# Three edge walks of a graph network with their hardware loops written out, and tile loads without bounds checks

## The chip, the cores and the metric

One core of one Trainium2 chip runs the whole program in a single launch. The metric is device time in microseconds (us) of that core. The kernel before took 7643.01 us in the median of 3 runs (7601.51 to 7684.22).

## What is computed

A graph of N = 3125 nodes (256 features each) and E = 53125 directed edges, self loops among them, goes through eight residual blocks, `x = x + block(layernorm(x))`: two graph convolutions, slice attention, graph attention (GAT), a mixture of experts, an edge update with a GRU, a second mixture, a relational convolution and a third mixture. The change touches two of them, graph attention and the edge update:

```
# graph attention, H = 4 heads of C = 64
h = (x @ W).reshape(N, H, C)
a_s = einsum('nhc,hc->nh', h, att_src);  a_d = einsum('nhc,hc->nh', h, att_dst)
e = leaky_relu(a_s[src] + a_d[dst], 0.2)
p = exp(e - segment_max(e, dst)[dst])
alpha = p / segment_sum(p, dst)[dst]
agg = segment_sum(h[src] * alpha[:, :, None], dst)

# edge update (row = src, col = dst)
msg = relu(concat(h[row], h[col], edge_attr) @ W1.T + b1) @ W2.T + b2
agg = segment_sum(msg, row)          # then a GRU over the nodes
```

## The kernel before

Nodes lie in 25 tiles of 128 (`NT`), a node per partition. The edges are sorted once by target node (and once by source, for the edge update) into WT = 440 columns of 128 slots; every column belongs to one node tile, whose number is read at run time from the rows `m.tn1` and `m.tn2`. The index of each slot's far node is in `m.src1`, its place within the tile in `m.lo1`.

An **edge walk** goes over the 440 columns in order, four (Q) at a time; such a four is a quad, and there are 110 (`QUADS`). Per column POOL gathers 128 rows of a table in DRAM by an indirect DMA, DVE builds a one-hot matrix from `lo1`, PE multiplies the one-hot matrix with the rows, so that the rows of each node are added up (or spread), and DVE adds or compares the result into the tile's place in SBUF. The engines run their own instruction streams, tied by semaphores; each has an order of steps written out by hand. The three walks that are changed:

- the **max walk** (lines 1408 to 1518) finds the greatest source score per node and head: POOL `gather` of `table_max` (L1453), ACT `masks` (L1436, L1439), PE `spread` (L1470, L1472), DVE `greatest` (L1501), `first_heads` (L1490), `hots` (L125), `keep` (L1512);
- the **sum walk** (1521 to 1677) weights and adds up the rows: POOL `gather` of `table_gat` (L1569), PE `turn_hots` (L1583), `scores` (L1592), `sums` (L1600), ACT `turned_hots` (L1550) and `numerators` (L1555), DVE `exponents` (L1641 to L1653), `weigh` (L1660, L1661), `add` (L1671);
- the **edge walk** (2116 to 2263) of the edge update: SP loads the slots' records, ACT copies their indices out (L2152), POOL gathers (L2183), PE `turn_in` (L2198, L2200), `inner` (L2211, L2212), `sums` (L2220), DVE `hots`, `mix` (L2249), `add` (L2258).

`pipeline(eng, ring, *steps)` (L143) orders one engine's steps. A step `(ahead, f)` is issued for quad q + ahead in the turn of quad q. The turns before quad 0 are written out; then a hardware loop (`Fori`) runs 110 // 8 - 1 = 12 rounds of 8 turns, in which quad numbers are register values, so that waits compare with a register and addresses are computed; the remaining 14 turns (quads 96 to 109) are written out with constants. In the attention walks ACT's step `indices`, six quads ahead, copies a quad's four index columns from `m.src1` at a register offset to a small ring `idx`, after PE is done with the quad eight before; POOL's `gather` waits for that copy, raises a semaphore `issue` that nobody waits for, and issues four gathers.

The node tile numbers come into registers through `node_tiles` (L163): one load of 8 numbers in every second quad for `NodeTiles` (DVE in all three walks, PE in the sum walk), one of 4 per quad for PE's `inner` in the edge walk. With each number goes a register instruction and an assert that check 0 to 24. `aggregate` (L612), which the graph convolutions (twice) and the relations use, is another edge walk, fully written out, with constant waits, indices read in place and tile numbers loaded through `tile_registers` (L605), without the checks.

Of the kernel before, what the change touches and what calls it, by code (L numbers as in the profile page):

```python
# [21 lines left out]
I32 = mybir.dt.int32  # L22
# [117 lines left out]
        return self.tiles[u % 2 * Q:(u % 2 + 1) * Q]  # L140


def pipeline(eng, ring, *steps, total=QUADS):  # L143

    rounds = total // ring - 1

    def turn_of(q):
        for ahead, step in steps:
            if 0 <= q + ahead < total:
                step(q + ahead, (q + ahead) % ring, (q + ahead) // ring)  # L150

    assert all(0 <= ahead <= ring for ahead, _ in steps)
    for q in range(-max(ahead for ahead, _ in steps), 0):
        turn_of(q)
    with eng.Fori(0, rounds) as i:
        for u in range(ring):
            for ahead, step in steps:
                step(i * ring + (u + ahead), (u + ahead) % ring, i + (u + ahead) // ring)
    for q in range(rounds * ring, total):
        turn_of(q)  # L160


def node_tiles(nc, eng, tn):  # L163

    return nc.values_load_multi_w_load_instructions(tn, engines=[eng.engine], min_val=0, max_val=NT - 1)[1]


def setup_memory(nc, ctx):
# [1151 lines left out]
def graph_attention(nc, m, a):  # L1320
# [85 lines left out]


    with Stage(nc) as st:
        names = ("indexed", "hot", "masked", "made", "topped", "bested", "issue", "initial")
        indexed, hot, masked, made, topped, bested, issue, initial = (st.sem(s) for s in names)  # L1410
        R, RS = 8, 4
        gathered = st.sems("gathered", R * Q)
        S = view(m.WS, 0, RS * Q, P)
        off = view(m.WS, RS * Q * P, RS * Q * P // 2).bitcast(BF16).rearrange("p (u e) -> p u e", e=P)
        o = RS * Q * P * 3 // 2
        rows = view(m.WS, o, R * Q, H)
        idx = view(m.WS, o + R * Q * H, R * Q).bitcast(I32)
        top = view(m.WS, o + R * Q * (H + 1), 2 * Q, H)
        minus = m.WS[:, o + R * Q * (2 * H + 1):o + R * Q * (2 * H + 1) + 1]
        diag = high[:, 0:RS * Q * H * P].rearrange("p (u h e) -> p u h e", u=RS * Q, h=H)  # L1420
# [2 lines left out]

        @block.scalar
        def _(act):
            def indices(j, u, r):
                act.wait_ge(made, j + 1)
                nc.scalar.copy(idx[:, u * Q:(u + 1) * Q], m.src1[:, bass.ds(j * Q, Q)]).then_inc(indexed, 1)

            def masks(j, u, r):  # L1430
                k = u % RS
                act.wait_ge(made, j + 1 + R - RS)
                for s in range(Q):
                    act.wait_ge(gathered[u * Q + s], r * 16 + 16)
                    for h in range(1, H):
                        nc.scalar.mul(diag[:, k * Q + s, h, :], m.ident[:], rows[:, u * Q + s, h:h + 1])  # L1436
                act.wait_ge(hot, j + 1)

                nc.scalar.activation(off[:, k * Q:(k + 1) * Q, :], S[:, k * Q:(k + 1) * Q, :], ACT.Identity,  # L1439
                                     bias=minus, scale=MASK).then_inc(masked, 1)  # L1440

            act.wait_ge(initial, 2)
            pipeline(act, R, (6, indices), (2, masks))

        @block.gpsimd
        def _(pool):
            nc.gpsimd.memset(minus, -MASK).then_inc(initial, 1)
            nc.gpsimd.tensor_copy(best, src_score).then_inc(initial, 1)
            def gather(j, u, r):
                pool.wait_ge(indexed, j + 1)  # L1450
                pool.sem_inc(issue, 1)
                for q in range(u * Q, (u + 1) * Q):
                    nc.gpsimd.indirect_dma_start(rows[:, q, :], None, m.table_max,  # L1453
                                                 bass.IndirectOffsetOnAxis(ap=idx[:, q:q + 1], axis=0)
                                                 ).then_inc(gathered[q], 16)

            pipeline(pool, R, (0, gather))

        @block.tensor
        def _(pe):  # L1460
            pe.sem_inc(made, R)

            def spread(j, u, r):
                k = u % RS
                pe.wait_ge(masked, j + 1)
                pe.wait_ge(topped, j + 1)
                for s in range(Q):

                    at = m.PS[:, u % 2 * Q + s, :]
                    nc.tensor.matmul(at, off[:, k * Q + s, :], m.identb[:].unsqueeze(1).to_broadcast([P, H, P]),  # L1470
                                     start=True, stop=False)
                    mm = nc.tensor.matmul(at, S[:, k * Q + s, :], diag[:, k * Q + s].rearrange("p h e -> p (h e)"),  # L1472
                                          start=False, stop=True)
                mm.then_inc(made, 1)

            pipeline(pe, R, (0, spread))

        @block.vector
        def _(dve):
# [25 lines left out]
            def keep(s):  # L1505

                def step(j, u, r):
                    if s == 0:
# [5 lines left out]


            node_tile, tiles = NodeTiles(nc, dve, m.tn1), [None] * Q
            pipeline(dve, R, (0, greatest), (2, first_heads), (0, keep(0)), (2, hots), (0, keep(1)), (0, keep(2)),
                     (0, keep(3)))


    with Stage(nc) as st:
        names = ("dstep", "ready", "own_diffed", "own_expd", "selfed", "indexed", "hot", "turned", "tcopied",
                 "scored", "taken", "estep", "diffed", "expd", "weighted", "summed", "added", "issue")
        (dstep, ready, own_diffed, own_expd, selfed, indexed, hot, turned, tcopied, scored, taken, estep, diffed,
         expd, weighted, summed, added, issue) = (st.sem(s) for s in names)
        R, RT = 8, 4
        gathered = st.sems("gathered", R * Q)
        S = view(m.WS, 0, R * Q, P)
        ST = view(m.WS, R * Q * P, RT * Q, P)
        o = (R + RT) * Q * P  # L1530
        idx = view(m.WS, o, R * Q).bitcast(I32)
        e, lk, p = (view(m.WS, o + (1 + k * H) * R * Q, R * Q, H) for k in range(3))
        own = view(m.WS, o + (1 + 3 * H) * R * Q, NT, H)
        rows = view(high, 0, R * Q, RW)
# [5 lines left out]

        @block.scalar
        def _(act):
            def indices(j, u, r):
                act.wait_ge(summed, (j + 1) * Q)
                nc.scalar.copy(idx[:, u * Q:(u + 1) * Q], m.src1[:, bass.ds(j * Q, Q)]).then_inc(indexed, 1)  # L1545
# [15 lines left out]
            pipeline(act, R, (6, indices), (4, turned_hots), (2, numerators))  # L1561

        @block.gpsimd
        def _(pool):
            def gather(j, u, r):
                pool.wait_ge(indexed, j + 1)
                pool.sem_inc(issue, 1)
                for q in range(u * Q, (u + 1) * Q):
                    nc.gpsimd.indirect_dma_start(rows[:, q, :], None, m.table_gat,  # L1569
                                                 bass.IndirectOffsetOnAxis(ap=idx[:, q:q + 1], axis=0)  # L1570
                                                 ).then_inc(gathered[q], 16)

            pipeline(pool, R, (0, gather))

        @block.tensor
        def _(pe):
# [29 lines left out]
            pipeline(pe, R, (2, scores), (0, sums), (4, turn_hots))  # L1606

        @block.vector
        def _(dve):
# [67 lines left out]
            pipeline(dve, R, (4, hots), (1, weigh), *mixed)  # L1677


    with Stage(nc) as st:  # L1680
# [417 lines left out]
def edge_update(nc, m, a):  # L2098
# [10 lines left out]
    def keep(dst):  # L2109
        return lambda t, ps: nc.vector.tensor_copy(tile_at(dst, t), ps)  # L2110
# [5 lines left out]
    CW = D + 1  # L2116
    with Stage(nc) as st:
        names = ("loaded", "oned", "indexed", "hot", "turned", "tcopied", "made", "mixed", "active", "summed",
                 "added", "issue")
        loaded, oned, indexed, hot, turned, tcopied, made, mixed, active, summed, added, issue = (  # L2120
            st.sem(s) for s in names)
        R, RS = 8, 4
        gathered, came = st.sems("gathered", RS * Q), st.sems("came", R)
# [14 lines left out]
        def _(sp):  # L2138
# [4 lines left out]
                sp.wait_ge(summed, (j + 1) * Q)  # L2143
                sp.dma_start(rec[:, u * Q:(u + 1) * Q, :], r[:, bass.ds(j * Q, Q), :]).then_inc(came[u], 16)

            pipeline(sp, R, (0, records))

        @block.scalar
        def _(act):
# [14 lines left out]
                nc.scalar.activation(rows[:, k, 0:D], rows[:, k, 0:D], ACT.Relu).then_inc(active, 1)  # L2164

            act.sem_inc(tcopied, 1)
            pipeline(act, R, (6, indices), (2, turned_in), (1, relu))

        @block.gpsimd
        def _(pool):  # L2170
# [6 lines left out]
            def gather(j, u, r):  # L2177
                pool.wait_ge(indexed, j + 1)
                pool.wait_ge(summed, (j + 1 + R - RS) * Q)
                pool.sem_inc(issue, 1)  # L2180
# [7 lines left out]
            pipeline(pool, R, (0, gather))  # L2188

        @block.tensor  # L2190
        def _(pe):
# [33 lines left out]
            pe.wait_ge(loaded, 16)  # L2225
            pe.wait_ge(oned, 1)
            pe.wait_ge(blanked, 2)
            pipeline(pe, R, (2, turn_in), (1, inner), (0, sums))

        @block.vector  # L2230
        def _(dve):
# [28 lines left out]
            dve.sem_inc(added, Q)  # L2260
            dve.sem_inc(mixed, 1)
            node_tile = NodeTiles(nc, dve, m.tn2)
            pipeline(dve, R, (3, hots), (1, mix), (0, add))


    sumsT = view(m.BB, 0, KD, NP)
# [745 lines left out]
```

## Time and profile before

| | |
|---|---|
| median of 3 runs | 7643.01 us (7601.51 to 7684.22) |
| the profiled execution | 7593.7 us, span 7591.9 us |
| PE busy | 5303.6 us (70%), mean granted clock 0.83 |
| DVE busy | 3536.6 us (47%) |
| POOL busy | 3390.8 us (45%) |
| ACT busy | 1465.3 us (19%) |
| max walk, sum walk, edge walk | 735, 775 and 770 us long |

The profile is of one execution. Times are us from the start of its span. A group's row gives busy time and mean ns of one instruction, then the idle time of the engine just ahead of it and what ended it; "issue" is idle time for which the profile shows no releaser. PEld is the weight load of a matmul. PEclk is the granted TensorE clock as a share of full speed (2.4 GHz). Register, branch and semaphore instructions have no rows of their own. The names of DMA releasers are those of an earlier stage that used the same semaphore, where stages share its number.

### The profile page before, as it was taken

What the parts mean: (1) busy time and instruction counts of PE and PEld (TensorE: products, weight loads), DVE (VectorE), ACT (ScalarE), POOL (GpSimd) and SP (SyncE); (2) the same over time, 40 slices, a digit from 0 to 9 for tenths busy, and PEclk for the clock granted to TensorE, in tenths of its full rate; (3) what the DMA queues carried; (4) which work ended last, traced back from release to release, by engine and by line L of the source; (5) the groups of instructions that cost most, each with busy time, mean ns of one, the idle gap of its engine ahead of it and who ended that gap; (6) DMA issues with size and microseconds to landing.
All of it is one profiled execution on the core that took longest, in us unless ns stands there. A gap on an engine that the chain in (4) does not pass through costs nothing. (4 is left out here: it accounts for less than half of the span.)

```text
span 7591.9 us, 94398 instructions
## 1 busy us (share of the span) xinstructions
PE 5303.6 (70%) x22797; PEld 3525.6 (46%) x22798; DVE 3536.6 (47%) x8494; ACT 1465.3 (19%) x3866; POOL 3390.8 (45%) x3530
## 2 busy tenths in 40 slices
PE   2665877677768477767776299479998549677645
PEld 0113555355535233335565188467776334355434
DVE  7874334333445466655556211355565632233412
ACT  0001000100032366631111122123333211000011
POOL 1714665466500266656662355335561030566322
PEclk9886888788889599977767599799999879788777
DMA  3102333233200000022321267323331043333245
GB/s 150 49 9 73 90 90 73 74 90 90 73 13 0 21 1 1 1 52 78 82 79 40 85 206 219 100 87 96 99 98 40 1 133 122 96 91 90 54 125 173
DMA packets 402907, 597.08 MB, mean 79 GB/s; under 512 B 131055, under 2 KB 305711, under 8 KB 401647
## 3 DMA queue, kind: packets, MB, share of 16 engines
q0 software_dynamic: 147584, 361.63, 17.2%
q1 hardware_dynamic: 255088, 232.69, 10.2%
q8 instruction: 103, 1.69, 0.1%
q14 instruction: 132, 1.08, 0.0%
HBM read 472.89 MB, written 121.17 MB: 78 GB/s over the span
## 5 line engine op out<-in xcount | busy, mean ns | idle before, releaser
L641 PE MATMUL ps<-zerow,zerob 128*128 128x256 bf16 x5280 | 966.1, 299 | 353.1 <-issue 301.4
L629 POOL DMA_INDIRECT wide<-table,src x880 | 884.1, 1005 | 733.5 <-ACTq L94 331.9
L671 DVE TENSOR_TENSOR sums<-sums,ps 128x256 f32 x1320 | 555.6, 421 | 1261.9 <-PE ps L644 775.2
L644 PE MATMUL ps<-wide 128*128 128x256 f32 x2640 | 947.2, 434 | 167.2 <-issue 152.1
L641 PEld LDWEIGHTS ps<-zerow,zerob 128*128 128x128 bf16 x5280 | 552.6, 107 | 749.4 <-issue 503.8
L629 POOL DMA_INDIRECT wide<-table_rel,rel x440 | 444.1, 1009 | 417.5 <-ACTq L94 217.6
L1569 POOL DMA_INDIRECT wide<-table_gat,work x440 | 469.6, 1067 | 309.9 <-ACT work L1545 174.2
L644 PEld LDWEIGHTS ps<-wide 128*128 128x128 f32 x2640 | 472.9, 217 | 277.8 <-issue 238.6
L2183 POOL DMA_INDIRECT work<-table,work x440 | 439.8, 999 | 306.0 <-PE ps L2220 158.2
L1453 POOL DMA_INDIRECT work<-table_max,work x440 | 432.9, 984 | 267.2 <-issue 138.7
L1472 PE MATMUL ps<-wide,work 128*128 128x512 f32 x880 | 499.5, 652 | 0.0
L1600 PE MATMUL ps<-wide,work 128*128 128x260 f32 x880 | 356.2, 562 | 91.5 <-DVE sums L1671 74.9
L1436 ACT ACTIVATE wide<-ident,work 128x128 f32<-128x128 f32 x1320 | 397.6, 387 | 4.3 <-DMA work<-table_max,work 4.0
L590 PE MATMUL ps<-ident,work 128*128 128x128 f32 x650 | 114.5, 341 | 368.2 <-ACT work L579 366.2
L1501 DVE TENSOR_REDUCE work<-ps 128x16 f32<-128x2048 f32 x110 | 252.0, 2291 | 194.6 <-issue 131.8
L486 POOL DMA_INDIRECT rec<-sums,record x256 | 248.5, 971 | 201.6 <-DMA sums<-in_edge_attr 128.6
L455 PE MATMUL ps<-wide 128*128 128x440 f16 x832 | 248.2, 392 | 113.7 <-DVE wide L431 55.3
L2211 PE MATMUL ps<-wide 128*128 x880 | 279.8, 401 | 60.2 <-DVE work L2249 36.6
L1671 DVE TENSOR_TENSOR sums<-sums,ps 128x260 f32 x440 | 186.7, 424 | 283.4 <-issue 100.8
L1470 PE MATMUL ps<-identb,work 128*128 128x512 bf16 x440 | 183.9, 418 | 191.8 <-ACT work L1439 170.0
L1600 PEld LDWEIGHTS ps<-wide,work 128*128 128x128 f32 x880 | 226.2, 277 | 164.7 <-DVE sums L1671 88.9
L579 ACT COPY work<-sums 128x256 f32 x100 | 33.6, 402 | 1378.9 <-PEq L583 1378.1
(431 smaller groups left out, 9347.1 us busy)
## 6 DMA issues: line engine op xcount, KB each, us to landing
wide<-in_L_ffn_W SPq DMA_DIRECT2D x64, 1024.0 KB
wide<-in_L_ffn_expert_w SPq DMA_DIRECT2D x90, 256.0 KB
table_rel<-wide SPq DMA_DIRECT2D x20, 1024.0 KB
work<-rows_in SPq DMA_DIRECT2D x62, 256.0 KB
rows_out<-work SPq DMA_DIRECT2D x62, 256.0 KB
work<-rec SPq DMA_DIRECT2D x110, 136.0 KB
wide<-table,src POOLq DMA_INDIRECT x880
rec<-work POOLq DMA_DIRECT2D x6, 2176.0 KB
```

Of the source, the lines that this page charges most:

```text
L629: nc.gpsimd.indirect_dma_start(rows[:, w % RT, :], None, table, bass.IndirectOffsetOnAxis(ap=index[:, w:w + 1], axis=0)).then_inc(gathered ...
L641: nc.tensor.matmul(m.PS[:, w % (2 * Q), 0:D], m.zerob[:, 0:P], m.zerow[:, 0:D], start=True, stop=True)
L644: nc.tensor.matmul(m.PS[:, w % (2 * Q), 0:D], S[:, w % RT, :], rows[:, w % RT, :], start=True, stop=True).then_inc(summed, 1)
L671: v.tensor_tensor(at, at, m.PS[:, s, 0:D], ALU.add).then_inc(added, 1)
L1436: nc.scalar.mul(diag[:, k * Q + s, h, :], m.ident[:], rows[:, u * Q + s, h:h + 1])
L1453: nc.gpsimd.indirect_dma_start(rows[:, q, :], None, m.table_max, bass.IndirectOffsetOnAxis(ap=idx[:, q:q + 1], axis=0)).then_inc(gathered[ ...
L1472: mm = nc.tensor.matmul(at, S[:, k * Q + s, :], diag[:, k * Q + s].rearrange("p h e -> p (h e)"), start=False, stop=True)
L1501: v.reduce_max(top[:, half * Q:(half + 1) * Q, :], m.PS[:, half * Q:(half + 1) * Q, :].rearrange("p s (h e) -> p s h e", h=H), AX).then_in ...
L1569: nc.gpsimd.indirect_dma_start(rows[:, q, :], None, m.table_gat, bass.IndirectOffsetOnAxis(ap=idx[:, q:q + 1], axis=0)).then_inc(gathered[ ...
L1600: te.matmul(m.PS[:, 4 + s, 0:RW], S[:, u * Q + s, :], rows[:, u * Q + s, :], start=True, stop=True).then_inc(summed, 1)
L2183: nc.gpsimd.indirect_dma_start(rows[:, k, 0:D], None, m.table, bass.IndirectOffsetOnAxis(ap=idx[:, u * Q + s:u * Q + s + 1], axis=0)).then ...
L2211: te.matmul(at, ST[:, k, :], tile_at(by_src, tiles[s]), start=True, stop=False)
```

## The change

`written_out` takes the place of `pipeline` in the three walks: the same turns in the same order, all 110 written out, so every quad number is a constant. `node_tiles` loads without the checks. In the attention walks ACT's step `indices`, the ring `idx` and the semaphores `indexed` and `issue` are gone, and POOL's gathers read their index column in `m.src1` itself. For the first eight quads a gather waits for nothing; later ones wait for the count that ACT's copy waited for. In the edge walk the index copy stays.

```diff
+def written_out(ring, *steps, total=QUADS):
+    for q in range(-max(ahead for ahead, _ in steps), total):
+        for ahead, step in steps:
+            if 0 <= q + ahead < total:
+                step(q + ahead, (q + ahead) % ring, (q + ahead) // ring)
...
 def node_tiles(nc, eng, tn):
-    return nc.values_load_multi_w_load_instructions(tn, engines=[eng.engine], min_val=0, max_val=NT - 1)[1]
+    return nc.values_load_multi_w_load_instructions(
+        tn, engines=[eng.engine], min_val=0, max_val=NT - 1,
+        skip_runtime_bounds_check_because="a count of node tiles started, ...")[1]
... (max walk)
-            def indices(j, u, r):
-                act.wait_ge(made, j + 1)
-                nc.scalar.copy(idx[:, u * Q:(u + 1) * Q], m.src1[:, bass.ds(j * Q, Q)]).then_inc(indexed, 1)
-
-            pipeline(act, R, (6, indices), (2, masks))
+            written_out(R, (2, masks))
             def gather(j, u, r):
-                pool.wait_ge(indexed, j + 1)
-                pool.sem_inc(issue, 1)
-                for q in range(u * Q, (u + 1) * Q):
+                if j >= R:
+                    pool.wait_ge(made, j + 1)
+                for s in range(Q):
+                    q, w = u * Q + s, j * Q + s
                     nc.gpsimd.indirect_dma_start(rows[:, q, :], None, m.table_max,
-                                                 bass.IndirectOffsetOnAxis(ap=idx[:, q:q + 1], axis=0)
+                                                 bass.IndirectOffsetOnAxis(ap=m.src1[:, w:w + 1], axis=0)
                                                  ).then_inc(gathered[q], 16)
-            pipeline(pool, R, (0, gather))
+            written_out(R, (0, gather))
-            pipeline(pe, R, (0, spread))
+            written_out(R, (0, spread))
... (DVE alike; the sum walk alike, with pool.wait_ge(summed, (j + 1) * Q); the edge walk:)
-            pipeline(sp, R, (0, records))
+            written_out(R, (0, records))
-            pipeline(act, R, (6, indices), (2, turned_in), (1, relu))
+            written_out(R, (6, indices), (2, turned_in), (1, relu))
             def gather(j, u, r):
                 pool.wait_ge(indexed, j + 1)
                 pool.wait_ge(summed, (j + 1 + R - RS) * Q)
-                pool.sem_inc(issue, 1)
-            pipeline(pool, R, (0, gather))
+            written_out(R, (0, gather))
-            pipeline(pe, R, (2, turn_in), (1, inner), (0, sums))
+            written_out(R, (2, turn_in), (1, inner), (0, sums))
-            pipeline(dve, R, (3, hots), (1, mix), (0, add))
+            written_out(R, (3, hots), (1, mix), (0, add))
```

## Rows read from the trace of the kernel before

**Rows 1.** Stretches of the max, sum and edge walks, and of a written-out walk.
```profile
core 0: us, PE busy (x) PEld busy (x) DVE busy (x) ACT busy (x) POOL busy (x), PEclk, DMA share, GB/s
2585.00:3320.00 735.00, 546.97 (x1320) 225.52 (x1320) 438.30 (x769) 474.65 (x1540) 433.19 (x442) 0.89 0.05 1
3330.00:4105.00 775.00, 549.20 (x2200) 433.30 (x2200) 440.58 (x1219) 100.13 (x331) 469.60 (x440) 0.71 0.30 77
4995.00:5765.00 770.00, 685.31 (x3521) 578.03 (x3522) 448.21 (x772) 236.33 (x443) 442.00 (x443) 0.96 0.34 95
6488.00:7135.00 647.00, 484.36 (x2513) 322.79 (x2514) 233.78 (x471) 0.00 (x0) 444.08 (x440) 0.82 0.33 90
```

**Rows 2.** Stretches, columns as before: looped, then written-out quads, of each walk.
```profile
2680.40:3191.70 511.30, 395.77 (x963) 163.41 (x962) 318.78 (x560) 345.04 (x1121) 315.06 (x321) 0.90 0.05 1
3241.50:3290.90 49.40, 38.88 (x97) 16.18 (x96) 31.43 (x56) 34.00 (x112) 30.65 (x31) 0.90 0.07 2
3421.00:3957.00 536.00, 398.60 (x1602) 315.46 (x1601) 312.39 (x881) 73.21 (x240) 337.40 (x321) 0.72 0.30 79
4014.40:4063.80 49.40, 38.74 (x156) 30.91 (x154) 30.88 (x89) 6.61 (x24) 33.15 (x33) 0.68 0.36 82
5070.10:5618.70 548.60, 498.32 (x2573) 420.98 (x2571) 325.90 (x561) 170.98 (x320) 320.56 (x321) 0.97 0.34 97
5672.90:5724.30 51.40, 46.81 (x246) 40.15 (x247) 32.13 (x56) 16.93 (x32) 31.68 (x32) 1.00 0.34 99
```

**Rows 3.** Timeline (start us, us, ...) of DVE's L1501: looped, then written-out quads.
```profile
3177.48 2.29 DVE L1501 TENSOR_REDUCE work<-ps 128x16 f32<-128x2048 f32 x1 [2.86 <-issue]
...
3191.76 2.29 DVE L1501 TENSOR_REDUCE work<-ps 128x16 f32<-128x2048 f32 x1 [3.81 <-issue]
...
3195.97 2.29 DVE L1501 TENSOR_REDUCE work<-ps 128x16 f32<-128x2048 f32 x1
...
3263.91 2.29 DVE L1501 TENSOR_REDUCE work<-ps 128x16 f32<-128x2048 f32 x1 [2.72 <-issue]
...
3272.84 2.29 DVE L1501 TENSOR_REDUCE work<-ps 128x16 f32<-128x2048 f32 x1 [4.67 <-PE ps L1472]
```

**Rows 4.** Groups of instructions of the max walk: POOL's gathers, ACT's index copies.
```profile
L1453 POOL DMA_INDIRECT work<-table_max,work x440 | 432.9, 984 | 267.2 <-issue 138.7 <-ACT work L1428 128.6
...
L1428 ACT COPY work<-src 128x4 int32 x96 | 17.0, 177 | 0.0
```

**Rows 5.** Waits in the sum walk: us in total, times, longest us.
```profile
POOL wide L1569 <- ACT work L1545: 174.2, 36, 45.5
```

**Rows 6.** Timeline of DVE: unchecked load in `aggregate`, checked load in the edge walk.
```profile
6809.14 1.22 DVE L125 TENSOR_TENSOR wide<-iota,lo 128x1024 f32<-128x1024 f32 x1
6811.77 0.42 DVE L671 TENSOR_TENSOR sums<-sums,ps 128x256 f32 x1 [1.42 <-issue]
...
5731.76 1.22 DVE L2249 TENSOR_TENSOR work<-work,ps 128x1024 f32<-128x1024 f32 x1 [2.71 <-DMA normed_T<-rows_out,back]
5734.83 0.42 DVE L2258 TENSOR_TENSOR sums<-sums,ps 128x257 f32 x1 [1.84 <-issue]
```

**Rows 7.** DMA queues: looped max walk; `aggregate`; last 91 us of the max walk.
```profile
q0 software_dynamic: 10829, 0.71, 4.8%
...
q8 instruction: 20, 0.33, 0.2%
q14 instruction: 14, 0.11, 0.1%
...
q14 instruction: 5, 0.04, 0.1%
```

**Rows 8.** Waits in `aggregate` (relations).
```profile
PE ps L641 <- issue: 101.3, 126, 3.1
...
POOL wide L629 <- PE ps L644: 56.1, 70, 2.8
...
POOL wide L629 <- DMA normed<-rows_out,back: 40.9, 31, 5.4
```

More of the change, by code:

```diff
@@ L163, in node_tiles @@
 def node_tiles(nc, eng, tn):
-    return nc.values_load_multi_w_load_instructions(tn, engines=[eng.engine], min_val=0, max_val=NT - 1)[1]
+    return nc.values_load_multi_w_load_instructions(
+        tn, engines=[eng.engine], min_val=0, max_val=NT - 1,
+        skip_runtime_bounds_check_because="a count of node tiles started, less one: tile 0 starts at slot 0, and there are NT")[1]
 def setup_memory(nc, ctx):
@@ L1408, in graph_attention @@
     with Stage(nc) as st:
-        names = ("indexed", "hot", "masked", "made", "topped", "bested", "issue", "initial")
-        indexed, hot, masked, made, topped, bested, issue, initial = (st.sem(s) for s in names)
+        names = ("hot", "masked", "made", "topped", "bested", "initial")
+        hot, masked, made, topped, bested, initial = (st.sem(s) for s in names)
         R, RS = 8, 4
@@ L1416, in graph_attention @@
         rows = view(m.WS, o, R * Q, H)
-        idx = view(m.WS, o + R * Q * H, R * Q).bitcast(I32)
         top = view(m.WS, o + R * Q * (H + 1), 2 * Q, H)
@@ L1516, in _ @@
             node_tile, tiles = NodeTiles(nc, dve, m.tn1), [None] * Q
-            pipeline(dve, R, (0, greatest), (2, first_heads), (0, keep(0)), (2, hots), (0, keep(1)), (0, keep(2)),
-                     (0, keep(3)))
+            written_out(R, (0, greatest), (2, first_heads), (0, keep(0)), (2, hots), (0, keep(1)), (0, keep(2)),
+                        (0, keep(3)))
     with Stage(nc) as st:
[L1522 to L1525, printed above, removed]
+        names = ("dstep", "ready", "own_diffed", "own_expd", "selfed", "hot", "turned", "tcopied",
+                 "scored", "taken", "estep", "diffed", "expd", "weighted", "summed", "added")
+        (dstep, ready, own_diffed, own_expd, selfed, hot, turned, tcopied, scored, taken, estep, diffed,
+         expd, weighted, summed, added) = (st.sem(s) for s in names)
         R, RT = 8, 4
@@ L1530, in graph_attention @@
         o = (R + RT) * Q * P
-        idx = view(m.WS, o, R * Q).bitcast(I32)
         e, lk, p = (view(m.WS, o + (1 + k * H) * R * Q, R * Q, H) for k in range(3))
@@ L1542, in _ @@
         def _(act):
-            def indices(j, u, r):
-                act.wait_ge(summed, (j + 1) * Q)
-                nc.scalar.copy(idx[:, u * Q:(u + 1) * Q], m.src1[:, bass.ds(j * Q, Q)]).then_inc(indexed, 1)
             def turned_hots(j, u, r):
@@ L1560, in _ @@
             nc.scalar.activation(own, own, ACT.Exp).then_inc(own_expd, 1)
-            pipeline(act, R, (6, indices), (4, turned_hots), (2, numerators))
+            written_out(R, (4, turned_hots), (2, numerators))
         @block.gpsimd
@@ L1565, in gather @@
             def gather(j, u, r):
-                pool.wait_ge(indexed, j + 1)
-                pool.sem_inc(issue, 1)
-                for q in range(u * Q, (u + 1) * Q):
+                if j >= R:
+                    pool.wait_ge(summed, (j + 1) * Q)
+                for s in range(Q):
+                    q, w = u * Q + s, j * Q + s
                     nc.gpsimd.indirect_dma_start(rows[:, q, :], None, m.table_gat,
-                                                 bass.IndirectOffsetOnAxis(ap=idx[:, q:q + 1], axis=0)
+                                                 bass.IndirectOffsetOnAxis(ap=m.src1[:, w:w + 1], axis=0)
                                                  ).then_inc(gathered[q], 16)
-            pipeline(pool, R, (0, gather))
+            written_out(R, (0, gather))
         @block.tensor
@@ L1605, in _ @@
             node_tile = NodeTiles(nc, pe, m.tn1)
-            pipeline(pe, R, (2, scores), (0, sums), (4, turn_hots))
+            written_out(R, (2, scores), (0, sums), (4, turn_hots))
         @block.vector
@@ L1676, in _ @@
             mixed = [f for n in range(4) for f in ((0, add(n)), (2, exponents(n)))]
-            pipeline(dve, R, (4, hots), (1, weigh), *mixed)
+            written_out(R, (4, hots), (1, weigh), *mixed)
     with Stage(nc) as st:
@@ L2118, in edge_update @@
         names = ("loaded", "oned", "indexed", "hot", "turned", "tcopied", "made", "mixed", "active", "summed",
-                 "added", "issue")
-        loaded, oned, indexed, hot, turned, tcopied, made, mixed, active, summed, added, issue = (
+                 "added")
+        loaded, oned, indexed, hot, turned, tcopied, made, mixed, active, summed, added = (
             st.sem(s) for s in names)
@@ L2179, in gather @@
                 pool.wait_ge(summed, (j + 1 + R - RS) * Q)
-                pool.sem_inc(issue, 1)
                 for s in range(Q):
@@ L2186, in gather @@
                     ).then_inc(gathered[k], 16)
-            pipeline(pool, R, (0, gather))
+            written_out(R, (0, gather))
         @block.tensor
```

## The prediction

> **What bounds the kernel now.** The page shows no engine busy for most of the span, so the bound has to be looked for stage by stage. The change touches three edge walks, two of attention and one of the edge update; the view by stretches shows them whole [rows 1]. The max walk takes 735 us with PE busy 547, the sum walk 775 with PE 549 at a granted clock of 0.71, the edge walk 770 with PE 685 (89%). The fourth stretch is a walk that the kernel already has written out with constant waits, `aggregate` on the table of relations: 647 us for the same 440 gathers.
>
> Each walk has 110 quads. 96 run in a hardware loop of 12 rounds of 8; the last 14 are already written out with constant waits, by the same functions. That is a sample of the new code inside the old trace. The stretches of rows 2 are cut at the start of one DVE instruction that comes once per quad (POOL's four gathers per quad show the count: x321 is 80 quads, x31 to x33 is 8). In the max walk 80 looped quads take 511.3 us, 6.39 each, and 8 written-out ones, with gathers still running, 49.4 us, 6.18 each. In the sum walk it is 6.70 against 6.18, in the edge walk 6.86 against 6.43 [rows 2].
>
> Who sets the pace: in the max walk the DVE chain. Once in two quads DVE stands ahead of L1501, 2.86 us in the loop and 2.72 written out: that is the load of eight node tiles with its checks. A quad without it takes 4.2 us from one L1501 to the next [rows 3], so two quads need 4.2 x 2 + 2.72 = 11.1 us, 5.6 each, and what is above that are other stops. It isn't POOL: gathers and the issue time between them are (432.9 + 138.7) / 110 = 5.20 us per quad, and POOL waits 128.6 us for ACT's index copies [rows 4], which come in step with the walk. In the edge walk PE is the bound, busy 498 of 549 us [rows 2]. In the sum walk no engine is near full, and POOL waits for ACT [rows 5]: its ring is paced by the waits between PE, DVE and ACT.
>
> **Part by part.**
> *Loops to constants.* Removed: the register arithmetic ahead of waits and addresses, and the branch of each round. Sum walk (6.70 - 6.18) x 96 = 50 us, edge walk (6.86 - 6.43) x 96 = 41. In the max walk the sample holds one stop of 4.67 us [rows 3]: with it the pace is 6.18, without it 5.6. I take 5.9, between the two: (6.39 - 5.9) x 96 = 47. Together 138. The bounds are 20 + 50 + 41 = 111 and 76 + 50 + 41 = 167.
>
> *Loads without checks.* DVE has 55 loads of eight tiles in each walk, and each tile loses a register instruction and an assert; PE loses the same in the sum walk (55 loads of eight) and in the edge walk (110 of four). No row of these walks shows an unchecked load. The nearest is in `aggregate`: eight tiles unchecked, behind a DVE instruction of 1.22 us, stand 1.42 us, where eight checked ones, also behind 1.22 us and also written out, stand 1.84 in the edge walk [rows 6]. So eight checks cost 0.42 us, and 55 times that 23. In the max walk DVE is the path: 23. In the sum walk I count one engine's loads, 23. In the edge walk PE is the path, 110 x 0.21 = 23, of which I take half, 12, since PE waits for DVE at the same place. Sum 58. The bounds are 0, if all of it lies beside other waits, and (2.72 - 1.42) x 165 = 215, if what follows no long instruction saves the whole difference.
>
> The Trainium skill (Runtime: NRT & Kernel Launch, "Instruction fetch mechanics") gives a register load about 200 ns per register, from HBM. By it the eight tiles would be 1.6 us of the 2.72 and the checks 1.1, and the change worth some 95 us more; no run here shows a bare load.
>
> *Index columns in place.* ACT loses 110 copies of 0.18 us in each attention walk [rows 4], 20 us of an engine busy 475 of 735 and 100 of 775 us [rows 1]: nothing. POOL pays nothing for the larger index array: in `aggregate`, which reads it so already, a gather is 444 / 440 = 1.01 us, against 0.98 in the max walk [rows 1]. What moves is the wait: a gather waits for PE's count itself and no longer for ACT's place in its queue, so POOL can be a full ring of eight quads ahead. In the sum walk it could start during the set-up, where it stands 45.5 us once [rows 5]. The pace is DVE's and PE's, so I take 0; the bound is 15 us gained, about what the set-up keeps it from. What its gathers could collide with is a DMA system busy 5 to 34% here [rows 1].
>
> *Small parts.* POOL's increment of a counter that nobody reads goes, 330 in all, beside POOL's own waits: 0. SP's record loads keep their place; their wait becomes a constant: 0.
>
> *Instruction supply*, which is added. In 540 us of the looped max walk POOL's queue has 10829 packets and no queue of kind instruction has any; the written-out `aggregate` has 20 + 14 such blocks in 647 us [rows 7]. There POOL, 32 gathers ahead, stands 56.1 + 40.9 = 97 us, and PE has 101 us of stops put to nothing but issue [rows 8]. The samples hold such fetches too (five blocks on one of the two queues in the last 91 us of the max walk [rows 7], with one stop of 4.67), but 8 quads are a thin sample. One such stop in 14 quads in the other two walks would be 0.33 x 96 x 2 = 64 us; I take half, 32 lost.
>
> Sum: 138 + 58 - 32 = 164 us. The profiled execution took 7593.7 us around a span of 7591.9, so it would take 7430. The median of the three runs is 7643.0, 49 above it, so the forecast is 7643 - 164 = **7479 us**. This case by itself: 7415 to 7545.
>
> **Rivals.**
> *Supply stalls take it all back (slower).* In `aggregate` 97 us for 34 blocks is 2.85 us a block. PE and its loads have 5027 records there and 2640, 4400 and 7043 in the three walks [rows 1], so PE's 20 blocks become 20 x 14083 / 5027 = 56, and with 14 of the other engines per walk there are 98: 98 x 2.85 = 279 us, less 138 + 58 = 196 gained, is 83 slower, 7726. It turns slower where more than 69 of the 98 blocks cost that much. For it: the rows of `aggregate`, and that PE in the edge walk has no slack to take a stop in. Against it: written out, the edge walk has PE busy 46.8 of 51.4 us at a clock of 1.00 [rows 2], as dense as PE's stream gets anywhere. The Trainium skill (same page and section) has sequential fetch hidden below the issue rate, and a taken branch that leaves the two fetched pages stall. By its first half this rival falls; by its second the loops would be fetching in every round, and rows 7 show no packet of that.
>
> *Half of it (within 1%).* A block costs 1.4 us: 196 - 137 = 59 faster, 7584.
>
> *More (clearly faster).* No stops, and the gathers' longer lead counts: the max walk at 11.1 - 0.4 per two quads, 5.35: (6.39 - 5.35) x 96 = 100; the sum walk at the same distance above POOL's floor as that, 5.6: 106; the edge walk at PE's busy time, 498 / 80 = 6.23: 60; 10 at the sum walk's start. 276 us, 7367. POOL's 5.20 lies under all three.
>
> *The change doesn't do what it says.* The tile loads themselves stay, and in the edge walk the index copy stays on ACT; the sums above have both in place.
>
> **How the numbers follow.** The forecast case has 0.55, clearly faster 0.18, half of it 0.15, slower 0.12. A measurement of this kernel tells a change from none at about 1%, 76 us. Slower by more than that is nearly the whole of the slow case, 0.10; within 1% are half of it and the edges of its neighbours, 0.16; faster is 0.74. The range, 7365 to 7625, holds the first three cases and leaves out the slow one and the upper bound of the checks.
>
> **What would show it.** The max walk from 735 to about 675 us, the sum walk from 775 to about 720, the edge walk from 770 to about 730. The stop ahead of L1501 falls to about 2.3 us; at 1.5 the checks were dearer than I say. ACT's index copies are gone from two walks. The three walks have about 100 instruction blocks. PE's stops for issue stay small; if POOL again stands about 100 us per walk for PE, the slow rival is right. PE's clock in the sum walk rises above 0.71; if it falls, stops have been added. The prediction is wrong if the written-out quads were quick only because one-hots and gathers run out near the end.

## The result, and the profile after

The changed kernel took 7449.74 us (median of 4 runs, 7376.91 to 7490.88) against 7658.94 for the kernel before: ratio 0.972, 95% interval 0.966 to 0.979. The forecast was 7479, 0.979 of the 7643 it started from. On a second chip the ratio was 0.977 (0.975 to 0.979). So the number was right, by luck: its split over the parts was not.

The stretches of the three walks after, which answer to [rows 1] (us, busy time and instructions of each engine, PE's granted clock, DMA share, GB/s):

```profile
2690.00:3355.00 665.00, 533.71 (x1320) 221.08 (x1320) 433.89 (x770) 460.94 (x1419) 434.71 (x435) 0.90 0.05 2
3378.00:4035.00 657.00, 495.97 (x2196) 367.95 (x2196) 420.37 (x1207) 84.60 (x220) 457.61 (x427) 0.77 0.34 87
4938.00:5646.00 708.00, 660.75 (x3509) 565.91 (x3509) 440.95 (x762) 234.50 (x435) 444.14 (x439) 0.99 0.37 103
```

ACT's instruction counts show the index copies gone from the first two. PE's clock in the sum walk rose from 0.71 to 0.77, as forecast. To compare walks I use one measure from here on: the time from the first to the last of the 110 DVE instructions that come once per quad (the reduce, the weighting, the mixing). It fell from 710 to 654 us in the max walk, 743 to 646 in the sum walk and 738 to 697 in the edge walk, 194 us together. The span of the profiled execution fell by only 112.4 (7591.9 to 7479.5). The difference lies ahead of the walks, in the placing of edges, whose code is the same. Its PE instructions (ns of one, first and last start in us) in five kernels: first in the kernel before and in the changed kernel,

```profile
L455 PE MATMUL ps<-wide x832: 348/359/575, 199.0 to 559.2; 128*128 128x440 f16 x167
```

```profile
L465 PE MATMUL ps<-wide x832: 349/359/574, 199.0 to 649.1; 128*128 128x440 f16 x167
```

then in the kernel before once more (e5), and in e12 and e10, two variants of the changed kernel that ran on one chip:

```profile
L455 PE MATMUL ps<-wide x832: 349/359/574, 198.8 to 485.3; 128*128 128x440 f16 x167
```

```profile
L465 PE MATMUL ps<-wide x832: 349/359/574, 199.4 to 486.0; 128*128 128x440 f16 x167
```

```profile
L465 PE MATMUL ps<-wide x832: 349/359/574, 199.2 to 558.9; 128*128 128x440 f16 x167
```

With the same code ahead of it and in it, the stage takes 287, 360 or 450 us in different executions (and 295 in e11); why isn't shown. So 90 us between the two profiles belong to no part of the change. Whole kernels are compared by the medians of their runs, each to the kernel before on its own chip; a walk is read from the one profile of its run. Where walks of the same code stand in two or more profiles of one chip, they differ by 1 us or less (the edge walk 713 and 712 in e5 and e7, 683 and 683 in e6 and e8, the sum walk 643 in e10 and e12). From chip to chip the walks of the kernel before differ by more: 688 to 710 us for the max walk.

POOL's gathers in the max walk after, and its waits in the edge walk (us in total, times, longest), which answer to [rows 4] and stand beside [rows 8]:

```profile
L1460 POOL DMA_INDIRECT work<-table_max,src x435 | 435.4, 1001 | 197.3 <-issue 128.0 <-remote 63.5 <-PE ps L1479 5.8
```

```profile
POOL work L2185 <- issue: 119.9, 359, 1.9
...
POOL work L2185 <- PE ps L2222: 97.7, 64, 4.0
```

POOL's wait for ACT of 128.6 us became 69 us of waiting for PE's count, the only one its code still waits for, under whichever name the trace gives the releaser. In the edge walk POOL does stand about 100 us for PE, the sign that the prediction gave to the slow rival, and the walk was faster all the same. The sign told nothing: in the kernel before the same wait was longer.

```profile
POOL work L2183 <- PE ps L2220: 158.2, 72, 6.6
```

### The profile page after: what moved, and what is told of

Its sections match the earlier page's. It is cut to its first block and busy times, and to the rows that moved or that the text cites. A ratio compares the mean times of both kernels' runs of the same rounds, so it can differ in the third digit from the quotient of the medians.

```text
span 7479.5 us, 84816 instructions
## 1 busy us (share of the span) xinstructions
PE 5204.9 (70%) x22797; PEld 3433.5 (46%) x22798; DVE 3518.6 (47%) x8494; ACT 1438.5 (19%) x3646; POOL 3398.1 (45%) x3530
## 3 DMA queue, kind: packets, MB, share of 16 engines
q0 software_dynamic: 147584, 361.63, 17.5%
## 5 line engine op out<-in xcount | busy, mean ns | idle before, releaser
L1572 POOL DMA_INDIRECT wide<-table_gat,src x440 | 475.1, 1080 | 214.2 <-issue 121.6
L1460 POOL DMA_INDIRECT work<-table_max,src x440 | 440.2, 1001 | 199.0 <-issue 129.6
L1603 PE MATMUL ps<-wide,work 128*128 128x260 f32 x880 | 320.7, 503 | 122.2 <-issue 67.6
L1603 PEld LDWEIGHTS ps<-wide,work 128*128 128x128 f32 x880 | 185.0, 237 | 209.3 <-issue 139.0
L600 PEld LDWEIGHTS ps<-ident,work 128*128 128x128 f32 x650 | 91.7, 172 | 393.4 <-ACT work L589 381.1
```

The source lines that it names most:

```text
L1603: te.matmul(m.PS[:, 4 + s, 0:RW], S[:, u * Q + s, :], rows[:, u * Q + s, :], start=True, stop=True).then_inc(summed, 1)
```

## The experiments

There are three theories of where the gain comes from. A, as predicted: the loops' register arithmetic, with the checks small and the index part nothing. B: the checks. C or D: the gathers' wait for the index copies. Walk times below are by the measure above; ratios are to the kernel before on the same chip. e1 to e4 ran on one chip, where the kernel before took 7434 us, e5 to e8 on another, where it took 7440. The chip of e1 to e4 has no profile of the kernel before, so their walks are set beside e5's from the other chip.

**e1, unchecked loads alone.**
```
 def node_tiles(nc, eng, tn):
-    ... min_val=0, max_val=NT - 1)[1]
+    ... min_val=0, max_val=NT - 1, skip_runtime_bounds_check_because="...")[1]
```


> The kernel before, with the node-tile loads unchecked and nothing else changed; all three walks stay looped. Measured is the pace between the per-quad DVE marker of quads 8 and 88 (6.39, 6.70 and 6.86 us in the max, sum and edge walk before; 5.82, 5.97 and 6.36 after the whole change) and the ratio. Theory A (the register arithmetic of the loops was the cost; the checks are small): 0 to 60 us off the whole, ratio 0.992 to 1.000; the max walk 6.2 to 6.4, the sum walk 6.5 to 6.7, the edge walk 6.7 to 6.9. Theory B (the checks were the cost: in a loop each is an instruction that must be fetched and run on the path): most of the some 200 us goes already here, ratio 0.975 to 0.985, max walk at 5.9 or less. Theory C (the gathers' index wait): no change at all.

Ratio 0.9955 (0.994 to 0.997), 33 us: B falls. A's range for the whole holds, its paces don't (6.50, 6.25 and 6.49 us a quad). The sum walk gained 36 us, but the max walk, where I had put the clearest gain, took 716 us against 688 in e5. That loss of 28 sets two chips side by side, and the kernel before varies by 22 from chip to chip, so its size isn't shown; a gain of 23 is not there.

**e2, written out alone.**
```
-            pipeline(pe, R, (0, spread))
+            written_out(R, (0, spread))
...
```


> The three walks written out with constant waits and nothing else: the loads keep their checks, ACT keeps its index copies and POOL its counter. Theory A: most of the gain, 110 to 190 us, ratio 0.975 to 0.985; the max walk at 5.9 to 6.2 us a quad, the sum walk 6.1 to 6.3, the edge walk 6.4. Theory B: under 60 us, ratio above 0.992. Theory C: the sum walk keeps its first eight quads at 70 us (54 after the change) and its pace above 6.4.

Ratio 0.9948 (0.993 to 0.9965): 39 us, where A asked for 110 to 190. The number is inside B's range, but e1 has ruled B out. The sum walk kept its first eight quads at 71 us, as C said, but not its pace: quads 8 to 88 went at 6.08, 6.20 and 6.37 us in the three walks. The profiled execution, the fastest of the four, was 25 us under their median, so the walks below make this part look dearer than the ratio does.

**e3, the changed kernel with the checks back.**
```
-        skip_runtime_bounds_check_because="..."
...
```


> The changed kernel with the checks put back in every node-tile load. Theory A: 0 to 60 us lost against the changed kernel, so a ratio of 0.972 to 0.982 to the kernel before; the stop ahead of reduce_max in a quad with a load, 2.7 us in the changed kernel, grows by at most 0.5. Theory B: it loses 100 us or more, ratio above 0.985, and that stop grows to 3.8 us, as 200 ns for each of the loaded registers or checks would make it.

Ratio 0.983 (0.981 to 0.985), some 46 us lost against the changed kernel (e6). That is A's loss, but the stop grew by more than A's 0.5 us. What the checks cost in place can be read off the reduce that follows a load of eight tiles. DVE's reduces in e3 (checked, written out), e2 (the same, with ACT's copies) and e4 (unchecked, with ACT's copies):

```profile
2924.82 2.29 DVE L1506 TENSOR_REDUCE work<-ps 128x16 f32<-128x2048 f32 x1 [2.72 <-issue]
2929.00 2.28 DVE L1506 TENSOR_REDUCE work<-ps 128x16 f32<-128x2048 f32 x1
```

```profile
2926.49 2.29 DVE L1509 TENSOR_REDUCE work<-ps 128x16 f32<-128x2048 f32 x1 [2.71 <-issue]
2930.91 2.29 DVE L1509 TENSOR_REDUCE work<-ps 128x16 f32<-128x2048 f32 x1
2937.90 2.29 DVE L1509 TENSOR_REDUCE work<-ps 128x16 f32<-128x2048 f32 x1 [2.72 <-issue]
2942.09 2.29 DVE L1509 TENSOR_REDUCE work<-ps 128x16 f32<-128x2048 f32 x1
2949.07 2.29 DVE L1509 TENSOR_REDUCE work<-ps 128x16 f32<-128x2048 f32 x1 [2.71 <-issue]
```

```profile
2899.65 2.29 DVE L1512 TENSOR_REDUCE work<-ps 128x16 f32<-128x2048 f32 x1 [0.50 <-issue]
2908.17 2.29 DVE L1512 TENSOR_REDUCE work<-ps 128x16 f32<-128x2048 f32 x1 [4.25 <-DMA wide<-table,src]
2912.95 2.29 DVE L1512 TENSOR_REDUCE work<-ps 128x16 f32<-128x2048 f32 x1 [0.50 <-issue]
2918.75 2.29 DVE L1512 TENSOR_REDUCE work<-ps 128x16 f32<-128x2048 f32 x1 [1.54 <-PE ps L1483]
2923.53 2.29 DVE L1512 TENSOR_REDUCE work<-ps 128x16 f32<-128x2048 f32 x1 [0.51 <-issue]
```

A load comes ahead of every second reduce. Checked, the stop behind it is never under 2.69 us in quads 8 to 95; unchecked it falls to 0.50. In the loops it is 2.86 at the least in e5 and 0.65 in e1. Eight checks are 2.2 us of DVE's time, not 0.42. And yet the walk did not get shorter by them: four quads take 22.6 us in e2 and 23.9 in e4, since the time saved comes back as waits of 4.25 and 1.54 us in the quads between. (The releaser "DMA wide" is a stale name of a reused counter.)

**e4, the changed kernel with ACT's index copies back.**
```
+            def indices(j, u, r):
+                act.wait_ge(made, j + 1)
+                nc.scalar.copy(idx[...], m.src1[...]).then_inc(indexed, 1)
...
-                if j >= R:
-                    pool.wait_ge(made, j + 1)
+                pool.wait_ge(indexed, j + 1)
```


> The changed kernel with ACT's index copies back in the two attention walks, written out, and POOL waiting for them. Theory A: max walk unchanged at 5.8 us a quad, the first eight quads of the sum walk back from 54 to 70 us, pace of the sum walk unchanged (5.97): 15 to 20 us lost, ratio 0.973 to 0.976. Theory C (the longer lead of the gathers set the pace): the max walk back to 6.1 or more and the sum walk to 6.3 or more, 60 us and more lost, ratio 0.980 and above.

Ratio 0.988 (0.985 to 0.991): Theory C's side, some 83 us lost against the changed kernel (e6). The max walk went to 6.28 us a quad, as C said, the sum walk to 6.14, short of C's 6.3.

**e5, the kernel before again; e6, the changed kernel again.**

> The kernel before once more, as it is, for its walks on the chip on which the next three run. Every theory: walks within 2% of 710, 743 and 738 us from first to last marker; what differs from the first profile lies in the placing of the edges ahead of the max walk (360 us in that profile), which the change does not touch.

> The changed kernel as it is, for the sum of the parts on one chip. If the parts simply add (23 us of checks, 64 of writing out, and some 85 of the direct index reads, from the four runs so far) it is 172 us faster than before, ratio 0.977. If the parts need each other (a stop taken from DVE only counts once the gathers come earlier) it is over 190 us, ratio under 0.9745.

e5's walks took 688, 726 and 713 us, 2 to 3% less than in the first profile, so the expectation of "within 2%" was missed: the same code differs that much from chip to chip. e6 has 0.977 (0.975 to 0.979), 173 us, as the sum of 172 said. But that sum was made along one order of putting the parts in, so that it came true doesn't show that each is worth the same alone. Their stretches (columns as above), first e5, then e6:

```profile
2517.00:3216.00 699.00, 536.17 (x1320) 221.28 (x1320) 436.15 (x767) 469.94 (x1523) 427.99 (x434) 0.91 0.05 1
3239.00:3976.00 737.00, 537.05 (x2192) 425.89 (x2192) 424.85 (x1203) 99.26 (x327) 463.16 (x439) 0.72 0.31 80
4882.00:5606.00 724.00, 663.75 (x3496) 563.73 (x3495) 439.86 (x756) 231.90 (x431) 435.65 (x436) 0.99 0.35 99
```

```profile
2519.00:3183.00 664.00, 531.85 (x1320) 220.65 (x1320) 433.78 (x769) 461.88 (x1421) 434.19 (x435) 0.90 0.05 2
3206.00:3853.00 647.00, 500.61 (x2196) 370.13 (x2196) 420.08 (x1207) 84.52 (x220) 457.30 (x427) 0.76 0.35 89
4754.00:5448.00 694.00, 656.18 (x3505) 564.65 (x3506) 439.57 (x761) 234.77 (x435) 443.69 (x439) 0.99 0.37 105
```

**e7, the index part alone, in the looped kernel.**
```
-            pipeline(act, R, (6, indices), (2, masks))
+            pipeline(act, R, (2, masks))
...
-            pipeline(pool, R, (0, gather))
+            written_out(R, (0, gather))      # reads m.src1 in place, waits for made
```


> The kernel before with the index part alone: POOL's gathers of the two attention walks read the index columns in place and wait for PE's count, written out on POOL; ACT's copies are gone; the other engines stay looped and their loads checked. Theory D (POOL's wait for ACT's copy held the gathers back, and these pace both walks): 60 to 90 us faster, ratio 0.988 to 0.992; POOL's 127 us of waiting in the max walk falls below 80. Theory A, as predicted (DVE's chain paces the max walk, the copies are hidden): 0 to 15 us, ratio 0.998 to 1.000; POOL then waits for PE as long as it waited for ACT.

Ratio 0.9965 (0.995 to 0.998), 26 us, between the two, so both D and A fall as they were written. The sum walk gained 54 us, the max walk lost 44, both against e5 on the same chip. POOL's wait in the max walk did not go, it grew, from 104 us for ACT in e5 to 148 here:

```profile
POOL work L1453 <- ACT work L1428: 104.1, 58, 10.2
```

```profile
POOL work L1458 <- PE ps L1477: 97.6, 26, 7.0
...
POOL work L1458 <- DMA wide<-table,src: 50.0, 23, 5.7
```

**e8, the place in ACT's queue without the copy.**
```
             def indices(j, u, r):
                 act.wait_ge(made, j + 1)
-                nc.scalar.copy(idx[...], m.src1[...]).then_inc(indexed, 1)
+                act.sem_inc(indexed, 1)
```


> The changed kernel, where POOL waits again for an increment that ACT makes at the old place in its queue, but ACT copies nothing and POOL reads the columns in place. Theory D (the place in ACT's queue is what costs): as slow as with the copies back, 60 to 90 us over the changed kernel, ratio to before 0.985 to 0.990, first eight quads of the sum walk at 66 us again. Theory E (the copies' own 0.18 us on ACT, whose masks are on the path, cost): within 20 us of the changed kernel, ratio 0.975 to 0.979.

Ratio 0.988 (0.986 to 0.990), the same as e4, and the first eight quads of the sum walk took 70 us. So in the written-out walks it is the way through ACT's queue that costs some 85 us, not the 0.18 us copies. Theory D holds there, E falls; in the looped kernel (e7) D's gain did not come. (The added step from PE over ACT to POOL and its place behind the masks come back together here; the waits of up to 8.2 us speak for the place.) POOL's wait in the max walk of e8:

```profile
POOL work L1463 <- ACTq L1437: 127.5, 33, 8.2
```

The total of POOL's waits isn't the price of the index part by itself: in the max walk of e2, with the copies in place, POOL waits 72 us for ACT, and in e3, without them, 75 us for PE, yet e3's walk is 19 us shorter.

The walks of these eight runs, in us, rounded, from first to last marker (e1 to e4 on one chip, e5 to e8 on the other):

| kernel | max | sum | edge | ratio |
|---|---|---|---|---|
| before (e5) | 688 | 726 | 713 | 1 |
| unchecked (e1) | 716 | 690 | 707 | 0.9955 |
| index direct (e7) | 732 | 672 | 712 | 0.9965 |
| written out (e2) | 681 | 692 | 695 | 0.9948 |
| written out, unchecked (e4) | 691 | 676 | 680 | 0.9879 |
| the same, place held (e8) | 701 | 670 | 683 | 0.9882 |
| written out, direct (e3) | 662 | 649 | 698 | 0.983 |
| all three (e6) | 653 | 636 | 683 | 0.9768 |

Single parts are worth 33 + 26 + 39 = 98 us, all together 0.0232 x 7440 = 173. The parts need each other, and two of them above all. Writing out and the direct index together (e3) give 0.0170 x 7440 = 126 us, 61 more than their 65 alone. Writing out and the unchecked loads together (e4) give 90, 18 more than their 72 alone, which is within the runs' intervals. The pair of direct index and unchecked loads in the loops was not run.

The last four ran on a third chip, on which the kernel before took 7520 us and walks of the same code are 0.4 to 3% longer than in e5 and e6.

**e9, still looped, three times as long a body.**
```
-    rounds = total // ring - 1
+    body = 3 * ring
+    rounds = (total // ring - 1) // 3
...
-        for u in range(ring):
+        for u in range(body):
```


> The kernel before, still looped in the three walks, but with 24 quads in a loop's body and 4 rounds in place of 8 quads and 12 rounds: a third of the branches, the same register arithmetic. Writing out alone took the walks from 688, 726 and 713 us to 681, 692 and 695, 59 us in all. Theory R (registers ahead of waits and addresses are what writing out removes): within 10 us of the kernel before, ratio 0.9985 to 1.0015. Theory J (the branch of each round, a stop of one to two us at the quad behind it): 36 branches of 3 walks become 12, two thirds of the gain, 35 to 45 us, ratio 0.994 to 0.9955. Theory F (a body three times as long has to be fetched again in every round): instruction packets in the hundreds and a slower kernel.

Ratio 1.006 (1.002 to 1.010). The walks took 712, 739 and 737 us; e11, whose max and sum walks are those of the kernel before, has 707 and 736. J's gain didn't come: a third of the branches gave nothing back. But it isn't clean, and the ratio lies outside R's range too. The three walks have 57 + 51 + 78 = 186 instruction blocks against 34 in e5, so the longer body is fetched again, as F said. R, with fetches that cost a little, can't be told from a branch gain that the fetches eat. Whether writing out removes the cost of the registers or that of the branches stays open.

**e10, more lead inside the max walk.**
```
-            written_out(R, (2, masks))
+            written_out(R, (3, masks))
...
-            written_out(R, (0, greatest), (2, first_heads), (0, keep(0)), (2, hots), ...
+            written_out(R, (0, greatest), (3, first_heads), (0, keep(0)), (3, hots), ...
```


> The changed kernel with DVE's first heads and one-hots and ACT's masks of the max walk three quads ahead of PE instead of two. Theory L (after the change the max walk is held by the chain PE, reduce, one-hots, mask, PE: DVE's one-hot of quad q + 2 is queued behind the reduce of quad q): the max walk falls from 653 towards POOL's own 439 + 124 = 563 us, to 570 to 620, 30 to 80 us off the whole, ratio to before 0.966 to 0.973. Theory G (the gathers' ring of eight quads holds it): one quad less of lead for the landing, 653 to 680 us, ratio 0.977 to 0.980.

The max walk took 650 us, against 656 in e12, whose max walk is the changed kernel's. L falls. G's range began at 653, and 6 us between two profiles decide nothing about it. Nor is this version shown to be a better one: its ratio is 0.974 (0.971 to 0.976), and the changed kernel's on another chip 0.977 (0.975 to 0.979). Lines of e10 show what is left. DVE stops some 4 us ahead of every third reduce: from 2824.43 to 2912.02 there are six such stops, 17.5 us apart, which is 5.84 us a quad, the walk's pace. At the last, POOL and DVE start again together, although PE's records, if I count its quads right, end the quad that both wait for at 2907.1. They start 0.6 and 0.9 us after the records end the next quad, at 2911.4; PE then stops for that reduce:

```profile
2859.36 2.29 DVE L1508 TENSOR_REDUCE work<-ps 128x16 f32<-128x2048 f32 x1 [3.87 <-PE ps L1479]
...
2876.88 2.29 DVE L1508 TENSOR_REDUCE work<-ps 128x16 f32<-128x2048 f32 x1 [4.28 <-PE ps L1479]
...
2906.06 1.02 PE L1479 MATMUL ps<-wide,work 128*128 128x512 f32 x2
...
2910.36 1.02 PE L1479 MATMUL ps<-wide,work 128*128 128x512 f32 x2
2912.02 2.29 DVE L1508 TENSOR_REDUCE work<-ps 128x16 f32<-128x2048 f32 x1 [4.38 <-PE ps L1479]
2912.26 0.95 POOL L1460 DMA_INDIRECT work<-table_max,src  x1 [1.97 <-PE ps L1479]
...
2914.46 0.58 PE L1477 MATMUL ps<-identb,work 128*128 128x512 bf16 x1 [3.08 <-DVE work L1508]
```

So the ring PE, reduce, PE sets the pace at 5.8 us a quad, over POOL's 5.1, with a wait in it that the records don't explain. Why the reduce starts one quad of PE's late stays open.

**e11 and e12, filler on PE in the edge walk, looped and written out.**
```
             def sums(j, u, r):
+                for f in range(24):
+                    pe.sem_inc(fill[f % 8], 1)
                 pe.wait_ge(active, j + 1)
```


> The kernel before, its edge walk still looped, with 24 semaphore increments more on PE per quad (2640, on counters that nobody reads). Only the price of issuing them: at 20 to 60 ns each 50 to 160 us, if none of it lies beside PE's stops. No instruction packets but those of the ends of the walk. This is the base for the next run.

> The changed kernel, its edge walk written out, with the same 24 increments more on PE per quad. It needs some 10 instruction blocks more on PE's queue than the 31 of the changed kernel. Theory S (each block is a stop of some 2.85 us, the slow rival of the prediction): it grows by 30 us or more above what the looped kernel grows by. Theory H (blocks arrive ahead of need): the edge walk grows by the same as in the looped kernel, within 10 us.

Looped (e11) the edge walk took 738 us. No run of this chip has the same loop without filler. Scaled from e5 by e10's 702 over e6's 683 it would be 733; the max walk's scale (707 over 688) would make it the same, the sum walk's (736 over 726) 723, and e9's longer loop took 737. Written out (e12) it took 725 against 702 in e10, 23 more. e11's ratio is 1.001 (0.997 to 1.006), far from the 50 to 160 us expected. e12's runs spread from 7351 to 7503 and gave no ratio. PE's queue (packets, MB, share) in e10's and e12's edge walk:

```profile
q8 instruction: 31, 0.51, 0.3%
```

```profile
q8 instruction: 41, 0.67, 0.4%
```

Ten blocks more, as expected. With the base of 733 the written-out walk grew by 23 - 5 = 18 us more than the loop, 1.8 us a block; with 737 and 723 it is 22 and 8 us, 2.2 and 0.8 a block. These are estimates, since the base is one. They lie between S (30 or more) and H (within 10), the lowest just inside H, and decide for neither: supply in the written-out edge walk may cost something, and less than the rival's 2.85 us.

## Why the prediction was right, and where it was wrong

*Loops to constants, 138 us: too large.* Written out alone (e2) the three walks gave 7 + 34 + 18 = 59 us, and 39 by the ratio. Writing out gave more where another part was there already: 26 + 14 + 27 us beside the unchecked loads (e1 to e4, one chip), and (0.9965 - 0.983) x 7440 = 100 us beside the direct index (e7 to e3). The step that failed is the sample of eight quads from one execution. The same reading of e5, the same kernel on another chip, gives (6.16 - 5.81) x 96 = 33 us, (6.60 - 6.46) x 96 = 13 and (6.55 - 6.22) x 96 = 31, together 77 and not 138. The last line of the prediction named another doubt, that the last quads are quicker than the same code is throughout. In e5 the 96th to 104th quads take 5.81, 6.46 and 6.22 us, where e2, written out from end to end, needs 6.08, 6.20 and 6.37: it held for two of the three walks, and explains less of the miss than the spread between executions.

*Loads without checks, 58 us: right in the sum, wrong in the mechanism.* Alone they gave 33 us, beside the written-out walks (e2 to e4) 51, last (e3 to e6) 0.0062 x 7440 = 46, of which 9 + 13 + 15 in the walks. In place, eight checks cost 2.2 us; the nearest row I chose, 1.42 against 1.84 in [rows 6], hid most of them behind other work. The upper bound of 215 assumed the whole difference; the true price was above even that row, (2.72 - 0.50) x 165 = 366 us of engine time. What failed is "in the max walk DVE is the path". With 2.2 us off that path per two quads, the max walk took 716 us in the looped kernel, where e5 has 688, and on one chip went from 681 to 691 in the written-out one. The Trainium skill (Runtime: NRT & Kernel Launch, "Instruction fetch mechanics") gives a register load 200 ns per register, which would be 1.6 us for the eight. It speaks of loads from HBM; these read SBUF, and the whole stop behind the unchecked load is 0.50 us, so the figure should not have been carried over to them.

*Index columns in place, 0 with a bound of 15: the largest miss.* Taken last it is 0.0111 to 0.0114 of 7440, 83 to 85 us (e4 and e8 against e6), in the walks 38 + 40; taken alone it is 26. Only the sum walk's start was seen (14 to 17 us of its first eight quads). The step that failed: "the pace is DVE's and PE's, so I take 0". POOL's 128.6 us of waiting for ACT [rows 4] and 174.2 [rows 5] were taken to come in step with a walk that something else paces. e8 shows that the place itself costs: ACT releases gather q + 6 only behind the masks of quad q + 1, and those wait for gathers and for DVE. A part put at nothing was thus about half of what the change brought.

*Instruction supply, 32 us lost.* In the stretches shown above 136 blocks came where about 100 were forecast, 39, 43 and 54 by walk. The slow rival needed 2.85 us for each of more than 69 of them; with all three parts the walks were 155 us faster, so it didn't come about. What the blocks cost was not measured by itself: no run shows the term of 32, and e12 leaves room for 0.8 to 2.2 us a block on PE. The prediction's sentence that the loops would be fetching in every round wants a longer body: with 8 quads in it the three walks have 34 blocks in e5, with 24 quads 186 in e9.

*The rivals.* The case "more" named the gathers' longer lead as a mechanism, but priced it by itself only at the sum walk's start, with 10 us; that mechanism, taken last, was about half of the 173, and the total was nearer to my 164 than to that case's 276. In the sum walk 90 us against 73 forecast, in the edge walk 30 against 53, in the max walk 35 against 70 (e5 to e6; the forecasts are those before the 32 for supply is taken off), and some 12 us outside the walks: an overestimate and an underestimate cancelled, which is luck. The first pair of profiles has 97, 41 and 57 us; how those split over the parts was not measured, since the parts ran on other chips.

## What to carry to other kernels

When several engines wait for one another in a ring, a wait that "comes in step" is not free: ask which queue place it depends on, and expect parts to be worth less alone (98 us) than together (173). Read a sample of new code from the middle of a walk and from more than one execution: eight quads of one gave 138 us, of another 77, and the measured part was 59. Read the cost of checks from the shortest stop behind such a load, not from one that lies beside other work.

## What the runs showed that I had not expected

The placing of the edges takes 287 to 450 us in different executions of the same code, more than most changes here are worth. Taking work off one engine can slow a ring: on one chip the max walk took 44 us more with gathers released directly (e7), and 10 more with cheaper loads (e2 to e4); POOL's waits in it rose from 104 to 148 us and from 72 to 102. Why the ring settles into a worse rhythm isn't shown. And 24 counter increments a quad on a PE that is over 90% busy made the written-out walk 23 us longer for 2640, 9 ns each, far below the 20 to 60 that I expected; some may lie beside PE's stops.
